# A two-layer graph kernel in batches: another order of the vector, scalar and GpSimd work for batches 0 to 3

## The chip, the cores and the metric

The kernel runs on one core of a Trainium2 chip. Its time is the device time of one execution in microseconds (us), the median of several executions; lower is better.

## The reference

```python
h = jnp.maximum(_layernorm(x, axis=-1), 0.0)          # x: (32, 256, 1024) float32
x = x + _L0_gnn_ref(h, adj, b1, adj, b2)               # adj: (256, 256), used as both weight matrices
...
    fv = x.mean(axis=1)                                # _construct_adj(h, 8), per batch
    nf = fv / norm(fv); sim = nf[:, :, None] * nf[:, None, :]
    _, idx = top_k(sim, 9); idx = idx[..., 1:]
    adj = zeros.at[b, row, idx].set(1.0); adj = max(adj, adj.T); adj[d, d] = 1
    ...
    h = relu(_gc(xr, adj, W1, b1)); h = _gc(h, adj, W2, b2)   # _gc: (adj / deg) @ (x @ W.T + b)
```

For each of 32 batches: layer norm and ReLU, a graph over the 1024 nodes built from the column means, and two graph convolutions with the same 256 x 256 weights, added to the input. The similarity is an outer product of one vector with itself, so a row of it picks either the largest or the smallest nodes; all nodes fall into 8 classes, and the graph is a small class-to-class table.

## The kernel before, in words

**Tiles.** A batch is two 128-row parts (`kf`, `m`) of 1024 columns, worked in two halves `h` of 512 columns. Float32 products are made from a high and a low part: `ps = w_hi*t_hi + w_lo*t_hi + w_hi*t_lo`, 8 matmuls in `product_hi` (L629) and 4 in `product_lo` (L635) for each half of each layer. The high part (`h_hi`, `r_hi`) is a ScalarE copy (`split_h` L366, `split_r` L403 and, for the very first half, L395), the low part (`h_lo`, `r_lo`) a GpSimd subtraction (L491, L502).

**One batch.** VectorE: statistics (`spreads` L761, `join` L768) and scale (`scales` L779, L782; `moments` is spreads and join). ScalarE: root of the variance (`root` L328), then the normalised `hb` (`normalise` L336). TensorE: `layer1`, then the graph's correction `masks` (L657, which reads the tile `onehot`). ScalarE: `relu` (L380 to L386), which also leaves column totals in `src2`. GpSimd: `products` (L481). VectorE: `class_terms` (L922). TensorE: `class_terms` (L688), VectorE: `table` (L928 to L934), which gives `tab`. TensorE: `layer2`, then `add_terms` (L664, reads `tab` and `onehot`). VectorE: `finish` (L943) adds bias and input, SyncE stores.

**Groups.** Batches go in groups of four that share the graph work: TensorE sums the columns of four normalised batches (`column_sums` L592; `first_sums` L579 for group 0), ScalarE copies the sums (`take_sums` L348 to L351) and makes the zero code (`zeros` L357 to L359, in the same PSUM tile `aux`), VectorE finds the top nodes (`top_first` L789 to `top_mark` L821), writes the class code (`codes` L827 to L831), `onehot` (L836) and its twin with the two 64-partition halves exchanged (`group_twin` L847, one call for each half), the degrees, factors, gathered rows, sources and biases (L856 to L915). GpSimd gathers rows of x by indirect DMA (`gather` L510) and builds `mix` (`tables`). `masks` of batches 0 and 1 need the first twin half of group 0, those of 2 and 3 the second.

**What sets the order.** Nothing is scheduled by a program. Each engine runs the calls in the order in which its function writes them, and semaphores hold an instruction until what it reads is there. From t = 3 on the loops repeat a fixed pattern with the statistics eight batches ahead; before that, batches 0 to 3 are written out by hand together with groups 0 and 1. TensorE's loop takes, for each t: `layer1(t+1, 0)` (with `class_terms(t)` between its two halves of products), `masks`, `add_terms(t, 0)`, `layer2(t, 1)`, `layer1(t+1, 1)`, `masks`, `add_terms(t, 1)`, `layer2(t+1, 0)`; for t = 0 the first `layer1` stands ahead of the loop, and `column_sums(1)` follows `add_terms(0, 1)`. `layer1(b, 1)` waits for `finish(b-1, 0)`, whose PSUM banks it takes over. `idle_products` (L696) are matmuls whose result nobody reads.

Of the kernel before, what the change touches and what calls it, by code (L numbers as in the profile page):

```python
# [19 lines left out]
H = 512  # L20
G = 4
# [71 lines left out]
def build(nc, x, x_t, w_t, b1, b2, small, staged, out):  # L93
# [5 lines left out]
    with ExitStack() as ctx:  # L99
# [225 lines left out]
        def _(act):  # L325
            def root(b):
                act.wait_ge(stats_ready, b + 1)
                nc.scalar.activation(std[:], mv[:, b % 2, :, 1], ACT.Sqrt, bias=eps[:]).then_inc(std_ready, 1)  # L328

            def normalise(b, kf):  # L330
                a, e = b % NH, b % RB
                if kf == 0:
                    act.wait_ge(norm_ready, b + 1)
                    if b >= NH:
                        act.wait_ge(hlo_ready, nth(b - NH, 1))
                last = nc.scalar.activation(  # L336
                    hb[:, a, kf], xin[:, b % NX, kf], ACT.Relu, bias=nmean[:, kf, e:e + 1],
                    scale=rstd[:, kf, e:e + 1], accum_out=h_tot[:, kf, e:e + 1])
# [15 lines left out]
            def zeros(k):  # L354
                com = dict(bias=half[:], scale=STEEP)
                act.wait_ge(fv_copied, 3 * k + 3)
                nc.scalar.activation(code[:, K_TOP + 1:H + 1], aux[:, K_TOP:H], ACT.Relu, **com)  # L357
                nc.scalar.activation(code[:, H + 1:N], aux[:, H:N - 1], ACT.Relu, **com)
                nc.scalar.activation(ZERO, aux[:, N - 1:N], ACT.Relu, **com).then_inc(zero_ready, 1)  # L359

            def split_h(b, h):
                n = half_of(h)
                act.wait_ge(h_ready, b + 1)
                if b > 0:
                    act.wait_ge(h_used, nth(b - 1, h))
                nc.scalar.activation(h_hi[:, :, n], hb[:, b % NH, :, n], ACT.Copy).then_inc(hhi_ready, 1)  # L366
# [53 lines left out]
            split_h(1, 1)  # L420
            normalise(5, 0)
            normalise(5, 1)
            first_unit()
            root(6)
            relu(0, 1, 0)
            relu(0, 1, 1)
            split_r(0, 1)
            normalise(6, 0)
            normalise(6, 1)

            for t in range(LAST):
                if t == 1:
                    normalise(LEAD + 1, 0)
                    normalise(LEAD + 1, 1)
                relu(t + 1, 0, 0)
                relu(t + 1, 0, 1)
                split_r(t + 1, 0)
                if t == 0:
                    root(7)
# [6 lines left out]
                if t == 0:  # L446
                    normalise(7, 0)
                    normalise(7, 1)
                    root(LEAD)
                if t == 1:  # L450
                    root(LEAD + 2)
                if 2 < t < NB - LEAD - 1:
# [4 lines left out]
                if t == 0:  # L457
                    take_sums(1)
                if t + 2 < NB:
                    split_h(t + 2, 1)  # L460
                if t == 0:
                    zeros(1)
                    normalise(LEAD, 0)
                    normalise(LEAD, 1)
                    root(LEAD + 1)
                elif t + LEAD + 1 < NB:
                    normalise(t + LEAD + 1, 0)
                    normalise(t + LEAD + 1, 1)
                if t == 1:
                    root(LEAD + 3)  # L470

        @block.gpsimd
        def _(pool):
# [72 lines left out]
            tables(0)  # L546
            split_h(1, 1)

            for t in range(-1, LAST):
                if t > 0 and (t + 1) % G == 0:  # L550
                    tables((t + 1) // G)
                if t == 1:
                    gather(1)
                split_r(t + 1, 0)
                if 1 < t < LAST - 1:
                    split_h(t + 2, 0, t + 1)
                else:
                    if t == 0:
                        split_h(2, 0)
                    products(t + 1)  # L560
                    if t == 1:
                        split_h(3, 0)
                split_r(t + 1, 1)
                if t >= 0 and t + 2 < NB:
                    split_h(t + 2, 1)
                if group_at(t, 0) is not None:
                    gather(group_at(t, 0))

        @block.tensor
        def _(pe):  # L570
# [182 lines left out]
        def _(dve):  # L753
# [220 lines left out]
            moments(6)  # L974
            spreads(7, 0)
            scales(6)
            spreads(7, 1)
            class_terms(0)
            join(7)
            spreads(8, 0)  # L980
            group_twin(0, 1)


            table(0)
            finish(0, 0)
            spreads(8, 1)
            scales(7)
            join(8)
            spreads(9, 0)
            spreads(9, 1)  # L990
            finish(0, 1)
            scales(8)
            join(9)
            spreads(10, 0)
            class_terms(1)
            spreads(10, 1)
            top_first(1)
            top_next(1)
            scales(9)
            join(10)  # L1000

            table(1)
            top_best(1)
            finish(1, 0)
            top_rows(1)
            spreads(11, 0)
            spreads(11, 1)
            finish(1, 1)
            scales(10)
            join(11)  # L1010
            top_mark(1)
            class_terms(2)

            table(2)
            finish(2, 0)
            codes(1)
            group_onehot(1)
            group_counts(1)
            group_twin(1, 0)
            group_twin(1, 1)  # L1020
            scales(11)
            finish(2, 1)
            group_degrees(1)
            group_factors(1)
            class_terms(3)
            group_gathered(1)
            group_sources(1)

# [64 lines left out]
```

## Time and profile before

| what | value |
|---|---|
| median of 3 executions | 502.77 us (502.76 to 504.25) |
| the profiled execution's own time | 504.29 us |
| its span, first to last instruction | 502.5 us |
| TensorE busy | 478.3 us (95%) |
| VectorE, ScalarE, GpSimd busy | 375.1, 350.0, 363.1 us (75%, 70%, 72%) |
| mean granted TensorE clock | 0.993 |

A span is what lies between the first and the last instruction; busy time is the union of an engine's instructions. "Idle before" in a row is how long the engine stood still just before it, and the releaser is the instruction for which it stood.

### The profile page before, as it was taken

What the parts mean: (1) busy time and instruction counts of PE and PEld (TensorE: products, weight loads), DVE (VectorE), ACT (ScalarE), POOL (GpSimd) and SP (SyncE); (2) the same over time, 40 slices, a digit from 0 to 9 for tenths busy, and PEclk for the clock granted to TensorE, in tenths of its full rate; (3) what the DMA queues carried; (4) which work ended last, traced back from release to release, by engine and by line L of the source; (5) the groups of instructions that cost most, each with busy time, mean ns of one, the idle gap of its engine ahead of it and who ended that gap; (6) DMA issues with size and microseconds to landing.
All of it is one profiled execution on the core that took longest, in us unless ns stands there. A gap on an engine that the chain in (4) does not pass through costs nothing.

```text
span 502.5 us, 7464 instructions
## 1 busy us (share of the span) xinstructions
PE 478.3 (95%) x2434; PEld 327.7 (65%) x2434; DVE 375.1 (75%) x956; ACT 350.0 (70%) x723; POOL 363.1 (72%) x343
## 2 busy tenths in 40 slices
PE   1997799899999999999999999999999999999996
PEld 0255556667776677767776677767777677777774
DVE  5989688988977898778877898878877675533334
ACT  4766698757877777777777777787777755556651
POOL 0356547957779687886888687896888687898883
PEclk9999799999999999999999999999999999999999
DMA  8992473556656465655656465664453244444424
GB/s 323 357 378 85 134 273 116 226 184 238 248 204 247 162 253 217 236 227 206 247 197 261 162 251 217 242 252 175 179 202 134 104 165 154 169 167 168 167 85 167
DMA packets 27718, 102.75 MB, mean 204 GB/s; under 512 B 2080, under 2 KB 2592, under 8 KB 27680
## 3 DMA queue, kind: packets, MB, share of 16 engines
q1 hardware_dynamic: 27296, 101.23, 53.5%
q0 software_dynamic: 384, 1.05, 0.6%
q8 instruction: 19, 0.31, 0.3%
q14 instruction: 19, 0.16, 0.1%
HBM read 68.72 MB, written 33.55 MB: 204 GB/s over the span
## 4 chain that ended last, share of the span: by engine, by line
PE 86%; DVE 5%; ACT 3%; DMA 3%; issue 1%; POOL 1%; SPq 0%; DVEq 0%; ACTq 0%; POOLq 0%
PE ps L629 48%; PE ps L635 22%; PE aux L592 5%; PE ps L657 4%; PE aux L688 3%; DMA xin<-x 2%; PE aux L616 1%; ACT hb L336 1%; PE aux L579 1%; DMA xg<-x_t,rows 1%; DVE res L943 1%; DVE onehot L847 1%; DVE stats L761 1%; PE aux L603 1%; POOL h_lo L491 1%
## 5 line engine op out<-in xcount | busy, mean ns | idle before, releaser
L502 POOL TENSOR_TENSOR r_lo<-r,r_hi 128x512 fp32r<-128x512 f32 x128 | 162.8, 1294 | 45.7 <-ACT r_hi L403 44.0
L491 POOL TENSOR_TENSOR h_lo<-hb,h_hi 128x512 fp32r<-128x512 f32 x128 | 164.0, 1295 | 7.5 <-ACT h_hi L366 7.4
L943 DVE SCALAR_TENSOR_TENSOR res<-ps,bias,res 128x512 f32<-128x512 f32 x128 | 90.1, 746 | 71.9 <-PE ps L664 71.9
L629 PE MATMUL ps<-r_hi,w_hi 128*128 128x512 f32 x256 | 109.0, 426 | 1.8 <-ACT r_hi L395 1.8
L629 PE MATMUL ps<-h_hi,w_hi 128*128 128x512 f32 x256 | 105.4, 412 | 0.4 <-DVE res L943 0.4
L629 PE MATMUL ps<-r_hi,w_lo 128*128 128x512 f32 x256 | 102.0, 399 | 0.0
L629 PE MATMUL ps<-h_hi,w_lo 128*128 128x512 f32 x256 | 101.0, 395 | 0.0
L336 ACT ACTIVATE hb<-xin,nmean,rstd 128x1024 f32<-128x1024 f32 x64 | 78.7, 1230 | 8.7 <-DVE nmean L782 8.7
L386 ACT ACTIVATE r<-ps,beta 128x512 f32<-128x512 f32 x64 | 43.4, 684 | 58.8 <-PE ps L657 56.5
L380 ACT ACTIVATE r<-ps,beta 128x504 f32<-128x504 f32 x64 | 43.5, 679 | 56.6 <-PE ps L657 52.3
L761 DVE BATCH_NORM_STATS2 stats<-xin 128x6 f32<-128x512 f32 x128 | 79.0, 677 | 3.6 <-DMA xin<-x 3.6
L635 PE MATMUL ps<-r_lo,w_hi 128*128 128x512 f32 x256 | 71.2, 400 | 0.0
L635 PE MATMUL ps<-h_lo,w_hi 128*128 128x512 f32 x256 | 70.2, 396 | 0.0
L403 ACT ACTIVATE r_hi<-r 128x1024 fp32r<-128x1024 f32 x63 | 66.8, 1061 | 2.4 <-PE ps L664 0.5
L629 PEld LDWEIGHTS ps<-r_hi,w_hi 128*128 128x128 f32 x256 | 48.5, 189 | 30.1 <-issue 12.9
L366 ACT ACTIVATE h_hi<-hb 128x1024 fp32r<-128x1024 f32 x64 | 67.0, 1047 | 0.0
L629 PEld LDWEIGHTS ps<-h_hi,w_hi 128*128 128x128 f32 x256 | 48.2, 188 | 17.8 <-issue 7.0
L635 PEld LDWEIGHTS ps<-r_lo,w_hi 128*128 128x128 f32 x256 | 48.4, 190 | 12.1 <-POOL r_lo L502 0.3
L635 PEld LDWEIGHTS ps<-h_lo,w_hi 128*128 128x128 f32 x256 | 48.1, 188 | 11.6
L629 PEld LDWEIGHTS ps<-h_hi,w_lo 128*128 128x128 f32 x256 | 48.3, 189 | 9.8
L629 PEld LDWEIGHTS ps<-r_hi,w_lo 128*128 128x128 f32 x256 | 48.7, 190 | 8.7
L481 POOL TENSOR_TENSOR prod<-src,mix 128x144 f32<-128x144 f32 x32 | 15.3, 478 | 48.8 <-issue 48.5
(100 smaller groups left out, 548.1 us busy)
## 6 DMA issues: line engine op xcount, KB each, us to landing
res<-x SPq DMA_DIRECT2D x32, 1024.0 KB, 4.9
out<-res SPq DMA_DIRECT2D x31, 1024.0 KB, 4.0
xin<-x SPq DMA_DIRECT2D x30, 1024.0 KB, 7.1
xin<-x SPq DMA_DIRECT2D x4, 512.0 KB, 5.0
out<-res SPq DMA_DIRECT2D x4, 256.0 KB, 2.1
w<-w_t SPq DMA_DIRECT2D x1, 256.0 KB, 9.0
cst<-small SPq DMA_DIRECT2D x1, 229.5 KB, 6.8
xg<-x_t,rows POOLq DMA_INDIRECT x8, 5.6
```

Of the source, the lines that this page charges most:

```text
L336: last = nc.scalar.activation(hb[:, a, kf], xin[:, b % NX, kf], ACT.Relu, bias=nmean[:, kf, e:e + 1], scale=rstd[:, kf, e:e + 1], accum_ou ...
L366: nc.scalar.activation(h_hi[:, :, n], hb[:, b % NH, :, n], ACT.Copy).then_inc(hhi_ready, 1)
L380: nc.scalar.activation(r[:, m, K_TOP:H], bank[m][:, K_TOP:H], ACT.Relu, accum_out=src2[:, m, e, C_COMMON:C_COMMON + 1], **com)
L386: last = nc.scalar.activation(r[:, m, H:N], bank[m][:], ACT.Relu, accum_out=src2[:, m, e, NCLS:NSRC], **com)
L403: nc.scalar.activation(r_hi[:, :, n], r[:, :, n], ACT.Copy).then_inc(rhi_ready, 1)
L491: last = nc.gpsimd.tensor_tensor(h_lo[:, kf, n], hb[:, b % NH, kf, n], h_hi[:, kf, n].bitcast(F32), ALU.subtract)
L502: last = nc.gpsimd.tensor_tensor(r_lo[:, kf, n], r[:, kf, n], r_hi[:, kf, n].bitcast(F32), ALU.subtract)
L592: last = nc.tensor.matmul(aux[32 * q:32 * q + 32, n], c_("ones")[:, 0:32], hb[:, (G * k + q) % NH, kf, n], start=(kf == 0), stop=(kf == KF ...
L629: nc.tensor.matmul(bank[m][:], wt[:, kf, m * P:m * P + P], mov[:, kf, n], start=(kf == 0 and wt is w_hi), stop=False, skip_group_check=True)
L635: last = nc.tensor.matmul(bank[m][:], w_hi[:, kf, m * P:m * P + P], mov[:, kf, n], start=False, stop=False, skip_group_check=True)
L761: last = nc.vector.bn_stats(stats[:, b % 2, kf, h], xin[:, a, kf, half_of(h)])
L943: nc.vector.scalar_tensor_tensor(res[:, b % NR, m, n], bank[m][:], bias2[:, m:m + 1], res[:, b % NR, m, n], ALU.add, ALU.add).then_inc(out ...
```

## The change

It touches batches 0 to 3 and groups 0 and 1; from t = 3 on every engine's order is as before. (In the changed file VectorE's lines are 43 higher, TensorE's 42 in the products, GpSimd's 35, ScalarE's 6.)

- The four `group_twin` calls of groups 0 and 1 leave VectorE; ScalarE makes these tiles by copying the other 64 partitions of `onehot` (`twin`).
- TensorE: in t = 0, `add_terms(0, 0)` moves from ahead of `layer2(0, 1)` to between its high and low products. Ahead of `layer2(0, 0)` there are four idle products of 256 columns instead of two, and two more behind its first two matmuls.
- ScalarE: `normalise(7)` moves ahead of `relu(1, 0)`, and `root`, `split_h`, `zeros` and `normalise` take other places.
- VectorE: statistics are dealt out otherwise; `table`, `finish` and the class work stand nearer to where they are read; `top_next` and `top_best` of group 1 go behind `finish(1, 0)`.
- GpSimd: `products(1)` goes ahead of `split_r(1, 1)`, `split_h(2)` behind it, and `gather(1)` behind `split_r(2, 1)` instead of ahead of `split_r(2, 0)`.

```diff
+            def twin(k, i):
+                act.wait_ge(counted, k + 1)
+                nc.scalar.activation(onehot[64 - 64 * i:128 - 64 * i, k % 2, 1], onehot[64 * i:64 * i + 64, k % 2, 0],
+                                     ACT.Copy).then_inc(onehot_ready, 1)
...
+            twin(0, 0)
             first_unit()
...
+            take_sums(1)
+            root(9)
+            split_h(2, 0)
+            split_h(2, 1)
+            zeros(1)
+            root(10)
+            twin(0, 1)
...
@@ GpSimd
+                split_r(t + 1, 1)
                 if t == 1:
                     gather(1)
...
@@ TensorE
                         if kf == 0 and m == 1 and rest is not None:
+                            idle_products(2, H // 2)
                             pe.wait_ge(rest, 1)
...
-            idle_products(2, H // 2)
+            idle_products(4, H // 2)
             layer2(0, 0)
...
                     masks(t + 1, 0)
+                    add_terms(t, 0)
+                    if group_at(t, 0) is not None:
+                        column_sums(group_at(t, 0))
+                    layer2(t, 1)
                 else:
                     terms()
-                add_terms(t, 0)
-                if group_at(t, 0) is not None:
-                    column_sums(group_at(t, 0))
-                layer2(t, 1)
+                    layer2(0, 1, lambda: add_terms(0, 0))
...
@@ VectorE
-            group_twin(0, 0)
+            spreads(6, 0)
             group_biases(0)
```

TensorE before, from the table's matmul of batch 0 on (`class_terms(0)`, `add_terms(0, 0)`, then `layer2(0, 1)`):

```order
L688 MATMUL aux<-w,src 24x128 x4
L664 MATMUL ps<-onehot,tab 128x512 x2
L629 MATMUL ps<-r_hi,w_hi 128x512
L629 MATMUL ps<-r_hi,w_lo 128x512
L629 MATMUL ps<-r_hi,w_hi 128x512
L629 MATMUL ps<-r_hi,w_lo 128x512
L629 MATMUL ps<-r_hi,w_hi 128x512
L629 MATMUL ps<-r_hi,w_lo 128x512
L629 MATMUL ps<-r_hi,w_hi 128x512
L629 MATMUL ps<-r_hi,w_lo 128x512
L635 MATMUL ps<-r_lo,w_hi 128x512 x4
```

The same place in the changed kernel:

```order
L730 MATMUL aux<-w,src 24x128 x4
L671 MATMUL ps<-r_hi,w_hi 128x512
L671 MATMUL ps<-r_hi,w_lo 128x512
L671 MATMUL ps<-r_hi,w_hi 128x512
L671 MATMUL ps<-r_hi,w_lo 128x512
L671 MATMUL ps<-r_hi,w_hi 128x512
L671 MATMUL ps<-r_hi,w_lo 128x512
L671 MATMUL ps<-r_hi,w_hi 128x512
L671 MATMUL ps<-r_hi,w_lo 128x512
L706 MATMUL ps<-onehot,tab 128x512 x2
L677 MATMUL ps<-r_lo,w_hi 128x512 x4
```

The two matmuls that read `tab` stand behind the eight high products.

VectorE before, from `class_terms(0)` to `finish(0, 0)`:

```order
L922 TENSOR_REDUCE src<-prod 128x48
L768 BN_AGGR mv<-stats 128x2 x2
L761 BN_STATS stats<-xin 128x6 x2
L847 TENSOR_SCALAR onehot,beside<-code_r,cst 64x1024
L928 CAST v_hi<-aux 128x128
L930 SCALAR_TENSOR_TENSOR aux<-v_hi,cst,aux 128x128
L932 CAST v_mid<-aux 128x128
L934 SCALAR_TENSOR_TENSOR tab<-v_mid,cst,aux 128x128
L943 SCALAR_TENSOR_TENSOR res<-ps,bias,res 128x512 x2
```

and now:

```order
L965 TENSOR_REDUCE src<-prod 128x48
L811 BN_AGGR mv<-stats 128x2 x2
L971 CAST v_hi<-aux 128x128
L973 SCALAR_TENSOR_TENSOR aux<-v_hi,cst,aux 128x128
L975 CAST v_mid<-aux 128x128
L977 SCALAR_TENSOR_TENSOR tab<-v_mid,cst,aux 128x128
L822 RECIPROCAL rstd<-std 128x2
L825 TENSOR_SCALAR nmean<-rstd,mv 128x1 x2
L986 SCALAR_TENSOR_TENSOR res<-ps,bias,res 128x512 x2
```

Two statistics and the twin are gone from ahead of the table; `scales(7)` stands behind it, ahead of `finish(0, 0)`.

ScalarE before, from `split_r(1, 1)` on (the sums of group 1, `split_h(2, 1)`, `zeros(1)`, batch 8):

```order
L403 ACTIVATE r_hi<-r 128x2x512
L348 ACTIVATE fv<-aux 128x512
L350 ACTIVATE fv<-aux 128x511
L351 ACTIVATE fv<-aux 128x1
L366 ACTIVATE h_hi<-hb 128x2x512
L357 ACTIVATE code<-aux,half 128x504
L358 ACTIVATE code<-aux,half 128x511
L359 ACTIVATE aux<-aux,half 128x1
L336 ACTIVATE hb,h_tot<-xin,nmean,rstd 128x1024 x2
```

and now:

```order
L409 ACTIVATE r_hi<-r 128x2x512
L348 ACTIVATE fv<-aux 128x512
L350 ACTIVATE fv<-aux 128x511
L351 ACTIVATE fv<-aux 128x1
L328 ACTIVATE std<-mv,eps 128x2
L372 ACTIVATE h_hi<-hb 128x2x512 x2
L357 ACTIVATE code<-aux,half 128x504
L358 ACTIVATE code<-aux,half 128x511
L359 ACTIVATE aux<-aux,half 128x1
L328 ACTIVATE std<-mv,eps 128x2
L364 ACTIVATE onehot<-onehot 64x1024
L336 ACTIVATE hb,h_tot<-xin,nmean,rstd 128x1024 x2
```

A root and one more half of `h_hi` now stand between the copied sums and the zeros, a root and the second twin half behind them.

## Rows read from the trace of the kernel before

**Rows 1.** The page: busy time of each engine, share of the span, instructions

```profile
PE 478.3 (95%) x2434; PEld 327.7 (65%) x2434; DVE 375.1 (75%) x956; ACT 350.0 (70%) x723; POOL 363.1 (72%) x343
```

**Rows 2.** Stretches of TensorE: busy us, matmuls, granted clock, DMA share, GB/s

```profile
0.00:103.90 103.90, 83.68 (x366) 0.97 0.63 231
150.00:497.00 347.00, 347.00 (x1823) 1.00 0.51 194
51.00:53.00 2.00, 0.00 (x0) 0.90 0.29 33
53.00:54.00 1.00, 0.76 (x3) 0.50 0.67 254
```

**Rows 3.** Timeline of TensorE, batch 0: start, us, line, count, idle before and releaser

```profile
42.85 1.13 PE L696 MATMUL aux<-hb,w 128*128 128x256 f32 x4
44.86 0.50 PE L629 MATMUL ps<-r_hi,w_hi 128*128 128x512 f32 x1 [0.87 <-ACT r_hi L395]
46.52 0.50 PE L629 MATMUL ps<-r_hi,w_hi 128*128 128x512 f32 x1 [0.93 <-ACT r_hi L395]
49.30 0.62 PE L688 MATMUL aux<-w,src 128*24 128x128 f32 x8 [0.18 <-DVE src L922]
53.24 0.61 PE L664 MATMUL ps<-onehot,tab 24*128 24x512 bf16 x2 [3.32 <-DVE tab L934]
59.06 0.57 PE L629 MATMUL ps<-h_hi,w_hi 128*128 128x512 f32 x1
```

**Rows 4.** Timeline of VectorE ahead of that table, and the first finish

```profile
50.59 1.28 DVE L847 TENSOR_SCALAR_CACHE_REDUCE onehot<-code_r,cst 64x1024 bf16<-64x1024 bf16 x1
51.80 0.28 DVE L928 CAST v_hi<-aux 128x128 bf16<-128x128 f32 x1
52.83 0.35 DVE L934 SCALAR_TENSOR_TENSOR tab<-v_mid,cst,aux 128x128 bf16<-128x128 bf16 x1
53.95 1.41 DVE L943 SCALAR_TENSOR_TENSOR res<-ps,bias,res 128x512 f32<-128x512 f32 x2 [0.77 <-PE ps L664]
```

**Rows 5.** Timeline of TensorE, group 1's sums and batches 1 to 3

```profile
62.46 3.64 PE L592 MATMUL aux<-hb,cst 128*32 128x512 f32 x32
69.95 0.62 PE L688 MATMUL aux<-w,src 128*24 128x128 f32 x8
72.57 0.39 PE L657 MATMUL ps<-onehot,mask 24*128 24x512 bf16 x2
73.76 0.39 PE L664 MATMUL ps<-onehot,tab 24*128 24x512 bf16 x2 [0.80 <-DVE tab L934]
76.97 0.40 PE L629 MATMUL ps<-h_hi,w_hi 128*128 128x512 f32 x1
79.87 0.39 PE L657 MATMUL ps<-onehot,mask 24*128 24x512 bf16 x2
79.88 0.39 PE L664 MATMUL ps<-onehot,tab 24*128 24x512 bf16 x2
97.52 0.47 PE L629 MATMUL ps<-h_hi,w_hi 128*128 128x512 f32 x1 [0.44 <-DVE res L943]
99.66 0.62 PE L688 MATMUL aux<-w,src 128*24 128x128 f32 x8 [0.98 <-DVE src L922]
```

**Rows 6.** Timeline of ScalarE: a root, a half of h_hi and the zeros of group 1, batch 4

```profile
46.37 0.28 ACT L328 ACTIVATE std<-mv,eps 128x2 f32<-128x2 f32 x1
66.71 1.06 ACT L366 ACTIVATE h_hi<-hb 128x1024 fp32r<-128x1024 f32 x1
67.66 0.69 ACT L357 ACTIVATE code<-aux,half 128x504 bf16<-128x504 f32 x1
68.79 0.25 ACT L359 ACTIVATE aux<-aux,half 128x1 f32<-128x1 f32 x1
103.79 0.68 ACT L380 ACTIVATE r<-ps,beta 128x504 f32<-128x504 f32 x1 [4.33 <-DVE beta L915]
```

**Rows 7.** Timeline of GpSimd: the low part of r for batch 0's second half

```profile
49.15 2.50 POOL L502 TENSOR_TENSOR r_lo<-r,r_hi 128x512 fp32r<-128x512 f32 x2 [0.55 <-ACT r_hi L403]
```

More of the change, by code:

```diff
@@ L428, in _ @@
             normalise(6, 0)
+            root(7)
             normalise(6, 1)
[L431 to L434, printed above, removed]
+            normalise(7, 0)
+            normalise(7, 1)
+            relu(1, 0, 0)
+            relu(1, 0, 1)
+            split_r(1, 0)
+            root(8)
+            relu(1, 1, 0)
+            relu(1, 1, 1)
+            split_r(1, 1)
+            take_sums(1)
[5 more added lines that the diff above has]
+            twin(0, 1)
+            normalise(8, 0)
+            normalise(8, 1)
+            relu(2, 0, 0)
+            relu(2, 0, 1)
+            split_r(2, 0)
+            split_h(3, 0)
+            normalise(9, 0)
+            relu(2, 1, 0)
+            relu(2, 1, 1)
+            split_r(2, 1)
+            split_h(3, 1)
+            normalise(9, 1)
+            normalise(10, 0)
+            relu(3, 0, 0)
+            relu(3, 0, 1)
+            split_r(3, 0)
+            split_h(4, 0)
+            normalise(10, 1)
+            relu(3, 1, 0)
+            relu(3, 1, 1)
+            root(11)
+            split_r(3, 1)
+            split_h(4, 1)
+            twin(1, 0)
+            normalise(11, 0)
+            normalise(11, 1)
+            twin(1, 1)
+            for t in range(3, LAST):
                 relu(t + 1, 0, 0)
@@ L437, in _ @@
                 split_r(t + 1, 0)
-                if t == 0:
-                    root(7)
                 if group_at(t, 0) is not None:
@@ L445, in _ @@
                     zeros(group_at(t, 0))
[L446 to L452, printed above, removed]
+                if t < NB - LEAD - 1:
                     root(t + LEAD + 1)
@@ L456, in _ @@
                 split_r(t + 1, 1)
-                if t == 0:
-                    take_sums(1)
                 if t + 2 < NB:
                     split_h(t + 2, 1)
[L461 to L466, printed above, removed]
+                if t + LEAD + 1 < NB:
                     normalise(t + LEAD + 1, 0)
                     normalise(t + LEAD + 1, 1)
-                if t == 1:
-                    root(LEAD + 3)
         @block.gpsimd
@@ L547, in _ @@
             split_h(1, 1)
-            for t in range(-1, LAST):
-                if t > 0 and (t + 1) % G == 0:
-                    tables((t + 1) // G)
+            split_r(0, 0)
+            products(0)
+            split_r(0, 1)
+            split_r(1, 0)
+            products(1)
+            split_r(1, 1)
+            split_h(2, 0)
+            split_h(2, 1)
+            for t in range(1, LAST):
+                if (t + 1) % G == 0:
+                    tables((t + 1) // G)
+                split_r(t + 1, 0)
+                if t < LAST - 1:
+                    split_h(t + 2, 0, t + 1)
+                else:
+                    products(t + 1)
+                split_r(t + 1, 1)
                 if t == 1:
                     gather(1)
[L554 to L564, printed above, removed]
+                if t + 2 < NB:
                     split_h(t + 2, 1)
@@ L971, in _ @@
             group_sources(0)
-            group_twin(0, 0)
+            spreads(6, 0)
             group_biases(0)
-            moments(6)
+            spreads(6, 1)
+            join(6)
             spreads(7, 0)
@@ L979, in _ @@
             join(7)
+            table(0)
+            scales(7)
+            finish(0, 0)
             spreads(8, 0)
-            group_twin(0, 1)
-            table(0)
-            finish(0, 0)
             spreads(8, 1)
-            scales(7)
             join(8)
             spreads(9, 0)
-            spreads(9, 1)
             finish(0, 1)
             scales(8)
+            spreads(9, 1)
             join(9)
@@ L995, in _ @@
             class_terms(1)
+            top_first(1)
+            scales(9)
             spreads(10, 1)
-            top_first(1)
-            top_next(1)
-            scales(9)
             join(10)
             table(1)
+            scales(10)
+            finish(1, 0)
+            top_next(1)
             top_best(1)
-            finish(1, 0)
             top_rows(1)
+            finish(1, 1)
+            class_terms(2)
+            top_mark(1)
+            table(2)
             spreads(11, 0)
[L1007 to L1014, printed above, removed]
             finish(2, 0)
@@ L1018, in _ @@
             group_counts(1)
-            group_twin(1, 0)
-            group_twin(1, 1)
+            spreads(11, 1)
+            join(11)
+            finish(2, 1)
+            class_terms(3)
             scales(11)
-            finish(2, 1)
             group_degrees(1)
             group_factors(1)
-            class_terms(3)
             group_gathered(1)
```

## Prediction, made before the changed kernel ran

> **What bounds the kernel now.** The page's busy times come first [rows 1]: TensorE works 95% of the span, the three others 70 to 75%, so a gain must come from TensorE's idle time or from its clock, and another engine's work counts only where TensorE stands for it. The stretches say where that is [rows 2]: from 150 to 497 us TensorE is busy for 347.00 of 347.00 us at full clock, while in the first 103.90 us it is busy for 83.68, which leaves 20.2 us idle. About half of that is the start, before the first matrix is there; the change leaves it alone. The rest is in batches 0 to 3, where the change is, and TensorE's timeline with its releasers gives it piece by piece: 0.87 and 0.93 us for ScalarE's r_hi, 3.32 us for VectorE's tab [rows 3], then 0.80 for tab, 0.44 for the finish of batch 2, 0.98 for the class sources of batch 3 [rows 5]. The clock matters too: in the wait for tab it falls from 1.00 to 0.50 of full speed, that is from 2.4 to 1.2 GHz [rows 2], and it is low for all of the unit of work that follows. As nothing in the loops is changed from t = 3 on and TensorE never waits there, a microsecond won or lost on TensorE before the fourth batch should arrive at the end unchanged. That is the frame of the sum.
>
> **The wait for tab, and the half clock.** TensorE finishes class_terms(0) at 49.30 + 0.62 = 49.92, and VectorE could start on the table then. It doesn't: statistics and a twin half stand in its queue, and the table runs from 51.80 to 52.83 + 0.35 = 53.18, 1.38 us [rows 4]. The change does two things here. VectorE has the table next, so tab is there at about 49.97 + 1.38 = 51.4. And TensorE doesn't wait for tab but does layer2(0, 1)'s eight high products first. They need r_hi of that half, which is there when GpSimd begins on it at 49.15; the low products need r_lo, ready at 49.15 + 2.50 = 51.65 [rows 7]. The same unit at full clock, terms and twelve products, takes 76.97 - 73.76 = 3.21 us [rows 5], its last third (four low products) about 0.95. So high products run from 49.92 to about 51.9, the terms find tab ready, and the low products find r_lo ready. The wait of **3.32** us is gone. So is the half clock, if it followed from that wait: the unit took 59.06 - 53.24 = 5.82 us [rows 3] against 3.21, which gives **2.61**.
>
> **Idle products.** Two of 256 columns begin at 42.85, and a pair lasts 1.13 us with its tail; two more end at about 45, just where r_hi arrives (44.86), and the pair behind the first two matmuls lies in the 0.93 us before 46.52 [rows 3]. They fill idle time: 0, at most 0.2 us of delay, and nothing gained unless the clock is spared by them.
>
> **The later waits.** In batch 1 the masks start at 72.57 and the terms at 73.76, while where tab is in time the two start together (79.87 and 79.88) [rows 5]. Tab was late by its own queue: the table of batch 1 follows statistics, roots and searches. In the new order VectorE has two statistics fewer to do there, joins are done earlier, and by my walk tab(1) is ready about half a microsecond before the masks. Gain 73.76 - 72.57 = **1.18**. The search of group 1 now goes behind finish(1, 0), the two twins (1.28 us each, as in [rows 4]) go to ScalarE and statistics of batch 11 are split around them, so finish(2, 1) and the sources of batch 3 come before TensorE asks: **0.44** and **0.98** gone. In the walk the sources are there 1.8 us ahead, the finish only some 0.5. Total removed: 3.32 + 2.61 + 1.18 + 0.44 + 0.98 = 8.53.
>
> **What is late next.** (1) layer1(1, 1) takes over the banks of finish(0, 0). Before, that finish (1.41 us, [rows 4]) lay beside layer2(0, 1). Now the terms that release it come late in the same unit: they end at 49.92 + 3.21 - 0.95 = 52.2, VectorE ends at about 53.65, TensorE asks at 53.13. With a semaphore's delay **0.55** us of wait; bounds 0 (its first matrix starts it earlier) and 1.4 (all of the finish). (2) class_terms(1) writes aux, so it waits for zeros(1). From the start T of group 1's column sums TensorE needs 69.95 - 62.46 = 7.49 us to reach it [rows 5]. ScalarE has copied the sums at T + 66.71 - 62.46 = T + 4.25; then come a root (0.28 at most), two halves of h_hi (0.95 each, 66.71 to 67.66) instead of one, and the zeros (67.66 to 69.04, 1.38) [rows 6]: T + 7.81. The wait is 0.32 and a semaphore, I take **0.4**; bounds 0 and 1.0, as ScalarE, which now has all of batch 7's normalising ahead of batch 1, could itself come late to the sums. (3) The biases of group 1 keep their place behind table(3), and the short wait of ScalarE and TensorE for beta stays.
>
> **The twin on ScalarE.** No row shows a copy of 64 x 1024 bf16. The nearest is L366's copy of 128 x 1024, 1.06 us; bounds 0.69 (half the columns, L357) and 1.28 (VectorE's). I take 1.06. The first falls before relu(0, 0), where ScalarE waits for TensorE; the last two fall where it stood 4.33 us before 103.79 [rows 6]. The one that can be felt is twin(0, 1), which masks(2, 0) needs: it ends near T + 9.2, TensorE asks at T + 7.89 + 72.57 - 69.95 = T + 10.5. Cost 0. The Trainium skill ("ScalarE: Activation LUTs", Rules for kernel authors) speaks against this move: in bf16 VectorE should be up to three times faster per element on such simple operations. The row has it otherwise: the form used here, with its sum, takes 1.28 us on VectorE, no less than ScalarE's copy. By the rule a third of 1.28, some 0.4, would be enough there, two twins would free VectorE of 0.9 us instead of 2.6, and the 1.8 us by which the sources of batch 3 are early would shrink to almost nothing: the sum would be the same or a few tenths less.
>
> **GpSimd.** gather(1) moves behind split_r(2, 1) and split_h(3, 1) moves behind the gather; both are read several microseconds later, and VectorE delivers the row numbers about when the queue gets there. Cost 0; if a gather came late, transposes in layer2(3, 0) would wait, which is a part of the third case below.
>
> **The sum.** 8.53 removed, 0.95 added: 7.6 us. Against its own span 502.5 - 7.6 = 494.9. The profiled execution took 504.29 us and lies 1.5 above the median of 502.77; the median is what is predicted, and 502.77 - 7.6 = **495.1 us**.
>
> **The rivals.**
> *The half clock stays, once.* TensorE's activity around 44 to 50 us is thin anyway [rows 3], and the clock could fall there or at the new wait at 53.1. Against it: gaps of 0.87, 0.93, 0.80 and 0.98 left it at 1.00 and only 3.32 us without work brought it down. Price: a unit at half clock, 2.6 us: 497.7.
> *Slower: short gaps bring the clock down each time.* This is one mechanism at the new waits near 53, 64 and at the beta wait. Each fall costs a unit at half clock, 2.6 us. Three give 7.8 and eat the gain (502.9); at a fourth, the first waits of batch 0, the kernel is slower, 505.5. The traced gaps speak against it. The Trainium skill ("TensorE: Matmul & The Clock Gate", A second HAM failure mode) describes such a kernel, where frequent small idle times between groups of matmuls made the clock swing; by that rule this case would rank higher, but the gaps of the trace don't bear it out.
> *A new wait in batches 1 to 3.* ScalarE or VectorE comes late by what the walk has wrong: twin(0, 1) past its 1.3 us, finish(2, 1) past its 0.5, a late gather. Price 1 to 3 us in all, say 2: 497.1.
> *No waits are added at all*: finish and zeros come in time, 494.1.
>
> **How the numbers follow.** Forecast 0.60 (494.3 to 496.3), nothing added 0.10, half clock once 0.10, a new wait 0.15, slower or level by the clock 0.05. The two shown clusters of executions are 1.5 us apart, which widens the top a little. Range 493.5 to 498.3: the low end is the sum without added waits and with a little more, the top a half-clock unit and half a microsecond. 0.3% is 1.5 us, about what a measurement of this kernel can tell from no change; every case but the clock's is below 501.3. Faster 0.95, same 0.02, slower 0.03.
>
> **What would show it.** Right: TensorE's row for tab in batch 0 without idle before it, granted clock 1.00 from 44 us on, a wait for a finish of about 0.5 us before layer1(1, 1), one of 0.4 for the zeros ahead of class_terms(1), no waits at the terms of batch 1 or the sources of batch 3, and group 2's column sums beginning near 96.3 where they began at 103.9 (the end of the first stretch in [rows 2]). TensorE should then be busy without a break as before. Wrong: any row of TensorE with over 1 us of idle after 50 us, a clock of 0.5 anywhere behind it, or new idle time in the loop from batch 4 on.

## The result, and the profile after

| | before | changed |
|---|---|---|
| median | 503.12 us (5 executions, 502.76 to 504.25) | 497.23 us (5 executions, 496.20 to 497.76) |
| ratio | | 0.9875, 95% interval 0.9863 to 0.9887 |
| profiled execution, its span | 504.29, 502.5 us | 497.13, 495.3 us |
| mean granted clock in it | 0.993 | 1.000 |

The change makes the kernel faster by 1.25%, 6.3 us (5.7 to 6.9) by the ratio; the two medians are 5.9 us apart. The forecast was 495.1 us in a range of 493.5 to 498.3, a gain of 7.6 us.

The page and the stretches of TensorE in the changed kernel (us busy, matmuls, clock, DMA share, GB/s), against [rows 1, 2]:

```profile
PE 476.9 (96%) x2442; PEld 327.1 (66%) x2442; DVE 371.3 (75%) x948; ACT 354.4 (72%) x727; POOL 364.2 (74%) x343
```

```profile
0.00:96.79 96.79, 82.31 (x374) 1.00 0.66 248
96.79:150.00 53.21, 53.21 (x276) 1.00 0.62 231
150.00:490.00 340.00, 340.00 (x1790) 1.00 0.51 192
```

Idle time ahead of group 2's column sums fell from 20.2 to 14.5 us, the clock stays at 1.00 in this execution (the other four have means of 0.997 to 0.999), and behind that point TensorE is busy without a break, as before. So what was won by then reached the end. TensorE's timeline of the changed kernel, the rows that answer to [rows 3, 5]:

```profile
49.64 0.62 PE L730 MATMUL aux<-w,src 128*24 128x128 f32 x8 [0.18 <-DVE src L965]
52.25 0.39 PE L706 MATMUL ps<-onehot,tab 24*128 24x512 bf16 x2
54.30 0.47 PE L671 MATMUL ps<-h_hi,w_hi 128*128 128x512 f32 x1 [0.53 <-DVE res L986]
65.44 0.62 PE L730 MATMUL aux<-w,src 128*24 128x128 f32 x8 [0.29 <-ACT aux L359]
68.06 0.39 PE L706 MATMUL ps<-onehot,tab 24*128 24x512 bf16 x2
94.92 1.08 PE L657 MATMUL aux<-src,w 128*128 128x32 f32 x8 [0.16 <-DVE src L942]
96.79 3.64 PE L633 MATMUL aux<-hb,cst 128*32 128x512 f32 x32 [0.18 <-DVE beta L958]
```

The wait for tab in batch 0 is gone, and so are those for batch 1's tab (68.06), for finish(2, 1) (0.44) and for batch 3's class terms (0.98). New are the waits for finish(0, 0) (0.53) and for the zeros (0.29), and one of 0.16 at the sources of group 1; the one at its biases is 0.18, where it was 0.43. From class_terms(0) to group 2's column sums it took 103.91 - 49.30 = 54.61 us before and takes 96.79 - 49.64 = 47.15 now: 7.46 us less. Of this, 5.10 us are won up to layer1(1, 1) (59.06 - 49.30 against 54.30 - 49.64) and 2.36 us behind it. The start was 0.34 us slower in this execution than in the profiled one of before.

VectorE's table and first finish, against [rows 4]:

```profile
50.31 0.29 DVE L971 CAST v_hi<-aux 128x128 bf16<-128x128 f32 x1 [0.54 <-PE aux L730]
51.35 0.35 DVE L977 SCALAR_TENSOR_TENSOR tab<-v_mid,cst,aux 128x128 bf16<-128x128 bf16 x1
52.74 1.41 DVE L986 SCALAR_TENSOR_TENSOR res<-ps,bias,res 128x512 f32<-128x512 f32 x2 [0.59 <-PE ps L706]
```

and ScalarE's first twin, its two halves of h_hi, the end of the zeros, and the second twin, against [rows 6]:

```profile
39.66 1.05 ACT L364 ACTIVATE onehot<-onehot 64x1024 bf16<-64x1024 bf16 x1
62.02 2.00 ACT L372 ACTIVATE h_hi<-hb 128x1024 fp32r<-128x1024 f32 x2
65.05 0.25 ACT L359 ACTIVATE aux<-aux,half 128x1 f32<-128x1 f32 x1
66.36 1.06 ACT L364 ACTIVATE onehot<-onehot 64x1024 bf16<-64x1024 bf16 x1
```

VectorE now waits for TensorE ahead of the table, where it used to begin the table 1.9 us after TensorE's last product. The twin copy takes 1.05 us on ScalarE, the 1.06 of the nearest row.

### The profile page after: what moved, and what is told of

It is laid out like the page before. It is cut to its first block, busy times and chain, and to the rows that moved or that the text cites. A ratio compares the mean times of both kernels' runs of the same rounds, so it can differ in the third digit from the quotient of the medians.

```text
span 495.3 us, 7476 instructions
## 1 busy us (share of the span) xinstructions
PE 476.9 (96%) x2442; PEld 327.1 (66%) x2442; DVE 371.3 (75%) x948; ACT 354.4 (72%) x727; POOL 364.2 (74%) x343
## 3 DMA queue, kind: packets, MB, share of 16 engines
q0 software_dynamic: 384, 1.05, 0.5%
## 4 chain that ended last, share of the span: by engine, by line
PE 82%; DVE 7%; ACT 4%; DMA 3%; issue 2%; POOL 1%; SPq 0%; DVEq 0%; ACTq 0%; POOLq 0%
PE ps L671 46%; PE ps L677 21%; PE aux L633 4%; PE ps L699 4%; PE aux L730 3%; DVE stats L804 2%; DMA xin<-x 2%; DVE res L986 1%; ACT hb L336 1%; PE aux L620 1%; PE aux L657 1%; DMA xg<-x_t,rows 1%; POOL h_lo L526 1%; PE aux L644 1%; ACT h_hi L372 1%
```

## The experiments

Ratios are to the kernel before, timed in the same session on the same chip. The runs lie in three sessions on three chips, and the changed kernel was timed in a session of its own (ratio 0.9875), so it is compared with the others through these ratios. A tenth of a per cent is 0.5 us. Each kernel ran 4 to 12 times.

**before_again**: no edit.

> The kernel before, unchanged, to see several of its executions with span and clock. Theory A (the gain of the change differs from the sum because the half-clock stretch in batch 0 is not equally long in every execution): mean granted clocks spread, say 0.993 to 1.000, and the executions with the higher clock are shorter by up to 2.6 us. Theory B (the spread comes from the start, from when the first loads land): the clock is the same in all, the spans differ by the start alone. Ratio to the kernel before 1.000.

Ratio 0.9999 (0.9986 to 1.0011). Twelve executions have spans from 500.6 to 503.3 us and mean clocks from 0.991 to 0.996. The four longest have 0.991, the eight others 0.993 to 0.996. Its profiled execution (span 501.2) is not the one that the prediction read. TensorE's timeline and stretches in it:

```profile
44.78 0.50 PE L629 MATMUL ps<-r_hi,w_hi 128*128 128x512 f32 x1 [0.87 <-ACT r_hi L395]
46.45 0.50 PE L629 MATMUL ps<-r_hi,w_hi 128*128 128x512 f32 x1 [0.93 <-ACT r_hi L395]
53.16 0.39 PE L664 MATMUL ps<-onehot,tab 24*128 24x512 bf16 x2 [2.02 <-DVE tab L934]
```

```profile
45.00:50.00 5.00, 4.07 (x11) 0.69 0.00 0
50.00:53.00 3.00, 1.14 (x10) 0.95 0.11 11
53.00:56.00 3.00, 2.84 (x8) 0.61 0.85 339
56.00:60.00 4.00, 4.00 (x16) 0.86 0.00 0
```

Here the clock fell twice: first behind the two waits of 0.87 and 0.93 us, then behind the wait for tab. The first fall cost nothing, since TensorE's slow work filled part of the time in which it would have waited: 2.02 us of wait instead of 3.32, and the terms begin at 53.16, where they began at 53.24 [rows 3]. The second fall cost less than the one in the first profile, since full speed came back sooner: layer1(1, 1) begins at 57.92, 4.76 us after the terms, not 5.82. This is 1.06 of the 1.3 us between the two spans. Against the 3.21 us of a unit at full clock, the half clock cost 1.55 us here and 2.61 there.

```profile
57.92 0.40 PE L629 MATMUL ps<-h_hi,w_hi 128*128 128x512 f32 x1
```

Theory A holds in that the falls differ between executions. The mean clock doesn't give the span (0.993 goes with 502.5 us in the first profile and with 501.2 here): a fall in front of a wait costs less than one behind it, and the mean also counts the end of the span, where TensorE has finished. In codes_early, below, no fall comes before 490 us, and yet its mean is 0.998:

```profile
492.00:494.50 2.50, 0.00 (x0) 0.58 0.64 242
```

How much of the spread of 2.7 us comes from the start (theory B) stays open, as only two of these executions have a trace.

**gap_filled**: idle products in the wait, written to banks that the next unit overwrites.

```diff
                 else:
                     terms()
+                    idle_beside(7)
                 add_terms(t, 0)
```

`idle_beside` (its definition is left out here) waits for r_hi of batch 0's second half and issues the given number of matmuls of 256 columns into the first bank of `pair2(0, 1)`.

> The kernel before, with seven idle products of 256 columns (some 3.15 us) put into TensorE's 3.3 us wait for tab in batch 0; nothing else. If the half clock follows from the wait, the clock stays at full speed and the unit behind it takes 3.2 us instead of 5.8: 2.6 us less, ratio 0.995, although the wait itself is as long as before. Rival (the clock falls on its own account around there, or the unit is slow for another reason): no change, ratio 1.000. If the idle products delay the terms, up to 0.3 us of it is lost.

Ratio 0.9968 (0.9956 to 0.9981): 1.6 us (1.0 to 2.2). The profiled execution has clock 1.000. Of the ten, seven have 0.999 to 1.000 and spans of 499.4 to 500.0 us, three have 0.997 and 501.1 to 501.3; these three have no trace. The clock is a term of its own, worth 1.6 us over all executions and not 2.6, which agrees with the 1.55 of the second profile. TensorE still can't go on before tab is there; seven products that nobody needs fill that time.

**terms_inside_only**: only TensorE's edit in t = 0 (the last TensorE part of the diff shown above).

> The kernel before, with TensorE's edit alone: add_terms(0, 0) between the high and the low products of layer2(0, 1). VectorE still delivers tab at 53.2, so TensorE works from 49.9 to 51.9 and waits 1.3 us instead of 3.3; the clock should hold. Gain 2.0 of waiting and 2.6 of half clock, less a wait of about 1 us for finish(0, 0) ahead of layer1(1, 1): some 3.7 us, ratio 0.993. Rival (the 1.3 us wait still brings the clock down): 1 us or less.

Ratio 0.9953 (0.9938 to 0.9968), 2.4 us, not 3.7. The wait for tab came as expected, the one for finish(0, 0) was half as long (0.53 instead of about 1), and the clock fell:

```profile
53.43 0.39 PE L664 MATMUL ps<-onehot,tab 24*128 24x512 bf16 x2 [1.25 <-DVE tab L935]
55.48 0.52 PE L629 MATMUL ps<-h_hi,w_hi 128*128 128x512 f32 x1 [0.53 <-DVE res L944]
```

```profile
55.00:56.00 1.00, 0.52 (x2) 0.89 1.02 418
56.00:59.00 3.00, 3.00 (x9) 0.50 0.02 5
```

In this execution two short waits close together, 1.25 and 0.53 us, were enough; two of the six have 0.999 and 1.000. So the edit on TensorE alone gives somewhat over a third of the change. Whether VectorE's new order or the added idle products are what keeps the clock in the change isn't shown by this run, as it has neither.

**no_idle_products**: the changed kernel without the idle products around layer2(0, 0).

```diff
-                            idle_products(2, H // 2)
...
-            idle_products(4, H // 2)
```

> The changed kernel without the four and the two idle products around the first matmuls of layer2(0, 0). If they only fill time in which TensorE waits for ScalarE, the time is that of the changed kernel (ratio 0.9875) or 0.1 us less. Rival (they are what keeps the clock up): gaps of 2.6 and 0.9 us stand there, the clock falls, and 1 to 3 us are lost, ratio 0.990 to 0.993.

Ratio 0.9903 (0.9887 to 0.9919), 1.4 us worse than the change, with intervals that just touch; all five executions have 0.992 or 0.994. Two waits of 1.93 and 0.76 us stand there. The clock falls behind the first of them, before the second begins, and is half for what follows:

```profile
44.35 0.50 PE L670 MATMUL ps<-r_hi,w_hi 128*128 128x512 f32 x1 [1.93 <-ACT r_hi L401]
46.01 0.79 PE L670 MATMUL ps<-r_hi,w_hi 128*128 128x512 f32 x1 [0.76 <-ACT r_hi L401]
```

```profile
44.00:45.00 1.00, 0.65 (x2) 0.88 0.00 0
45.00:50.00 5.00, 4.24 (x10) 0.50 0.00 0
50.00:53.00 3.00, 3.00 (x16) 0.74 0.25 22
```

**before_idle_products**: the same products put into the kernel before.

```diff
+                            idle_products(2, H // 2)
                             pe.wait_ge(rest, 1)
...
-            idle_products(2, H // 2)
+            idle_products(4, H // 2)
```

> The kernel before with the idle products of the change alone: four ahead of layer2(0, 0) and two behind its first two matmuls. If the clock in the kernel before falls in some executions already at the 0.87 and 0.93 us waits for r_hi (as in the second profile of it, near 46 us), this takes that fall away and leaves the one at the wait for tab; as the first fall lies partly in the shadow of the wait for tab, the gain is small: 0 to 0.7 us, ratio 0.9985 to 1.000. Rival (the idle products carry the gain of the change): ratio 0.995 or less.

Ratio 1.0008 (0.9995 to 1.0021). With the wait for tab behind them they bring nothing: in this trace too the clock falls in that wait of 3.32 us (0.64 in the stretch from 52 to 53 us, 0.50 from 53 to 56). They are worth 1.4 us in the changed kernel, which has no such wait.

**terms_ahead**: the changed kernel with add_terms(0, 0) ahead of layer2(0, 1).

```diff
-                    layer2(0, 1, lambda: add_terms(0, 0))
+                    add_terms(0, 0)
+                    layer2(0, 1)
```

> The changed kernel with add_terms(0, 0) back ahead of layer2(0, 1). TensorE then waits from 50.3 to 51.7 for tab (1.4 us), without a fall of the clock; finish(0, 0) comes earlier, so the wait of 0.5 us ahead of layer1(1, 1) goes. Loss 0.9 us against the changed kernel, ratio 0.989. Rival (the clock falls in the 1.4 us): loss 3 us or more, ratio 0.994.

Ratio 0.9882 (0.9868 to 0.9897), which isn't resolved from the change's own. Its profiled execution shows a wait of 1.50 us for tab and then a fall:

```profile
51.00:52.00 1.00, 1.00 (x6) 0.98 0.00 0
52.00:55.00 3.00, 3.00 (x9) 0.50 0.96 321
```

In that trace the way from class_terms(0) (48.60) to group 2's sums (97.76) takes 49.16 us, 2.0 more than in the changed kernel. The start was 1.04 us quicker in the same execution, which hides half of it. The other three executions have 0.998 and 0.999, too high for a stretch as long as this one (over 3 us at half clock), so that the fall is the exception there. The expected 0.9 is inside the interval, and the rival's 3 us isn't, though the fall that it named did come once; the size between 0 and 1.1 stays open.

**gather_ahead**: GpSimd's gather back ahead of split_r(2, 0).

```diff
+                if t == 1:
+                    gather(1)
                 split_r(t + 1, 0)
...
                 split_r(t + 1, 1)
-                if t == 1:
-                    gather(1)
```

> The changed kernel with gather(1) back ahead of split_r(2, 0) in GpSimd's queue. VectorE gives the row numbers at 75.0, so r_lo(2, 0) is ready at 78.6 instead of 75.7, and TensorE, which asks at 76.5, waits 2 us: ratio 0.992. Rival (the gather's place is without effect, something else is late there anyway): ratio 0.9875 as the changed kernel.

Ratio 0.9915 (0.9902 to 0.9928), 2.0 us worse, as expected. TensorE's row says for what:

```profile
78.25 2.02 PE L677 MATMUL ps<-r_lo,w_hi 128*128 128x512 f32 x4 [2.30 <-POOL r_lo L537]
```

In this execution the clock fell behind that wait too (mean 0.996); the four others have 1.000 and took 0.6 to 0.9 us less.

VectorE's long operation of codes(1), of which more below, happens to fall into a pause of GpSimd here:

```profile
86.36 1.21 DVE L870 SCALAR_TENSOR_TENSOR code_r<-fv,code 128x1015 bf16<-128x1015 f32 x1
```

```profile
83.55 2.52 POOL L526 TENSOR_TENSOR h_lo<-hb,h_hi 128x512 fp32r<-128x512 f32 x2
88.26 2.56 POOL L537 TENSOR_TENSOR r_lo<-r,r_hi 128x512 fp32r<-128x512 f32 x2 [2.19 <-ACT r_hi L409]
```

**twins_back**: group 1's two twin halves made by VectorE again.

```diff
             group_counts(1)
+            group_twin(1, 0)
+            group_twin(1, 1)
             spreads(11, 1)
```

> The changed kernel with the two twin halves of group 1 made by VectorE again, behind group_counts(1). Each takes 1.28 us there; in the changed kernel the sources come 0.16 us late for TensorE as it is, so the full 2.6 us are added ahead of them: ratio 0.993. Rival (there is slack in VectorE's queue there, as the prediction had it with 1.8 us): at most 0.8 us, ratio 0.989.

Ratio 0.9932 (0.9919 to 0.9945), 2.9 us worse, about the length of both (2.55 us). The wait that grows is that for finish(2, 1), which stands behind them in VectorE's queue, ahead of the sources; the sources themselves then come in time:

```profile
93.12 0.67 PE L669 MATMUL ps<-h_hi,w_hi 128*128 128x512 f32 x1 [2.18 <-DVE res L984]
```

So finish(2, 1) had about 0.4 us to spare in the changed kernel (2.55 - 2.18). The clock fell behind that wait in this execution (0.50 from 94 to 96 us), but the one execution with 1.000 took no less than the others (500.13 us against a median of 500.30).

**both_waits** takes the two new waits away; **bank_by_bank** has the first of its edits alone.

```diff
+                        if kf == 0 and m == 1 and second is not None:
+                            pe.wait_ge(out_ready, second)
...
+                elif b == 1 and h == 1:
+                    pe.wait_ge(out_ready, 1)
                 elif b > 0 and h == 1:
                     pe.wait_ge(out_ready, 2 * nth(b - 1, 0))
...
             split_h(2, 0)
-            split_h(2, 1)
             zeros(1)
+            split_h(2, 1)
```

> The changed kernel with two of its own new waits taken away: layer1(1, 1) waits for the first bank of finish(0, 0) only and for the second ahead of its third matmul, and zeros(1) goes ahead of split_h(2, 1) on ScalarE. If the waits are what the rows say (0.53 and 0.29 us) and nothing takes their place, 0.8 us less than the changed kernel, ratio 0.986. Rival (the time is handed to the next wait, sources or biases of group 1, whose VectorE queue is full from 83 us on): 0.3 us or less.

Ratio 0.9959 (0.9944 to 0.9973): 4.2 us slower than the change. Both waits are gone from TensorE's rows (one of 0.23 us for twin(0, 1) takes the place of a part), and the loss comes some 30 us later. VectorE's main operation of codes(1) took 3.02 us in the changed kernel and takes 6.75 here:

```profile
82.33 6.75 DVE L874 SCALAR_TENSOR_TENSOR code_r<-fv,code 128x1015 bf16<-128x1015 f32 x1
```

GpSimd in the same stretch:

```profile
81.70 2.56 POOL L526 TENSOR_TENSOR h_lo<-hb,h_hi 128x512 fp32r<-128x512 f32 x2
84.21 2.53 POOL L537 TENSOR_TENSOR r_lo<-r,r_hi 128x512 fp32r<-128x512 f32 x2
86.70 1.29 POOL L526 TENSOR_TENSOR h_lo<-hb,h_hi 128x512 fp32r<-128x512 f32 x1
88.27 1.12 POOL L516 TENSOR_TENSOR prod<-src,mix 128x144 f32<-128x144 f32 x1 [0.28 <-issue]
```

and ScalarE's r_hi(3, 0), which the pair at 84.21 reads:

```profile
82.74 1.06 ACT L409 ACTIVATE r_hi<-r 128x1024 fp32r<-128x1024 f32 x1
```

GpSimd runs five subtractions without a pause, from 81.70 to 87.99. VectorE's operation, begun at 82.33 by the trace, ends at 89.08, 1.1 us after the pause begins. In the changed kernel the same two engines look like this:

```profile
82.97 3.02 DVE L870 SCALAR_TENSOR_TENSOR code_r<-fv,code 128x1015 bf16<-128x1015 f32 x1
```

```profile
82.35 2.56 POOL L526 TENSOR_TENSOR h_lo<-hb,h_hi 128x512 fp32r<-128x512 f32 x2
84.86 3.53 POOL L537 TENSOR_TENSOR r_lo<-r,r_hi 128x512 fp32r<-128x512 f32 x2
```

```profile
83.70 1.06 ACT L409 ACTIVATE r_hi<-r 128x1024 fp32r<-128x1024 f32 x1
```

There r_hi(3, 0) is ready at 84.76, just as GpSimd gets to it (84.86); VectorE gets through between GpSimd's two pairs (the seam, below), and GpSimd's second pair is 1.0 us longer instead. In both_waits r_hi is ready at 83.80, 0.4 us before GpSimd gets to it: ScalarE is earlier by more than GpSimd, the seam closes, and VectorE stands until the next pause. Four traces go together here: a margin of 0.1 us and 3.02 us of operation in the changed kernel and in twins_back, 0.4 us and over 6.7 in both_waits and bank_by_bank. No run moves r_hi alone, so that its timing decides at the seam is argued from these four. Late counts then cost 0.64 and 0.89 us on TensorE, a late finish(2, 1) 1.47, and the clock falls:

```profile
93.76 0.77 PE L673 MATMUL ps<-h_hi,w_hi 128*128 128x512 f32 x1 [1.47 <-DVE res L990]
```

```profile
94.00:95.00 1.00, 1.00 (x3) 0.50 0.48 193
```

The fall isn't the main loss: three of the six executions have a clock of 1.000 and still took 500.95 to 501.36 us, the three others 501.90 to 502.68.

> The changed kernel with layer1(1, 1) waiting for finish(0, 0) bank by bank, the other wait left as it is. TensorE is 0.5 us earlier from 54 us on. If codes(1) keeps its 3 us, ratio 0.9865; if ScalarE's earlier r_hi takes away the gap between GpSimd's subtractions, the operation takes 5 us or more and the ratio is 0.992 or more. The theory of a race against that gap allows both and says that the time follows the length of that one operation; the rival says that time and that length have nothing to do with one another.

Ratio 0.9946 (0.9930 to 0.9962), and the operation takes 6.76 us. This edit alone closes the seam: r_hi(3, 0) is ready at 84.37, and GpSimd gets to it at 84.79.

**codes_early** and **both_waits_codes**: codes(1) moved on VectorE, in the changed kernel and in both_waits.

```diff
             table(2)
-            spreads(11, 0)
+            codes(1)
             finish(2, 0)
-            codes(1)
+            spreads(11, 0)
             group_onehot(1)
```

> The changed kernel with codes(1) on VectorE moved from behind finish(2, 0) to behind table(2), and spreads(11, 0) from ahead of finish(2, 0) to behind it. Theory (the long operation of codes(1), 3.0 us in the changed kernel and 6.75 us with both waits taken away, is held back by GpSimd's subtractions and gets through where GpSimd pauses): started near 80.5 it falls into the pause in which GpSimd issues the gather (81.2 to 82.3) and takes 1.2 to 2 us; the sources' and biases' waits of 0.16 and 0.18 us go: ratio 0.9868, 0.3 us less than the changed kernel. Rival (the operation is slow for what it reads, wherever it stands): still 3 us, ratio 0.9875.

Ratio 0.9845 (0.9832 to 0.9859), median 496.32 us. The operation is held for the last 0.7 us of a subtraction pair and then falls beside the gather, where GpSimd has no subtraction running:

```profile
80.07 1.79 DVE L870 SCALAR_TENSOR_TENSOR code_r<-fv,code 128x1015 bf16<-128x1015 f32 x1
```

```profile
78.24 2.54 POOL L537 TENSOR_TENSOR r_lo<-r,r_hi 128x512 fp32r<-128x512 f32 x2
80.94 1.80 POOL L545 DMA_INDIRECT xg<-x_t,rows  x1 [0.16 <-issue]
```

> Both waits taken away as before, and codes(1) moved as in the kernel beside it. Theory (GpSimd's hold on that one operation was the whole loss of 4.4 us): the operation takes 1.2 to 2 us, no clock falls near 92, and the time is 0.8 to 1.1 us below the changed kernel: ratio 0.9855. Rival (one of the two edits costs by itself, such as half of h_hi too late): ratio 0.992 or more, as with both edits alone.

Ratio 0.9849 (0.9835 to 0.9863), median 496.57. With the operation in the pause, the same two edits that had cost 4.2 us cost nothing: the hold of GpSimd on it was the loss. They bring no more than 0.1 us over codes_early, though: from class_terms(0) to group 2's sums it is 46.62 us against 46.73, and 47.15 in the changed kernel. What they save comes back as a wait of 0.23 us for twin(0, 1) at masks(2, 0), one of 0.17 at class_terms(2), and small delays at the sources and biases. The expected ratio, 0.9855, is inside the interval, but the trace has only 0.53 us less than the changed kernel's where 0.8 to 1.1 was expected. Of the lower median of codes_early, 0.9 us below the changed kernel's, 0.38 is the start in the traced pair; codes_early is the fastest version found, with an interval that only just clears that of the change.

## Why the prediction was right, and where it was off

**The frame** held: nothing from group 2's sums on changed, and the 7.46 us won ahead of them are, but for 0.1 us, what the profiled spans show once the start is set apart (502.5 - 495.3 = 7.2, plus 0.34 of slower start). The sum of 7.6 us was right for this pair of executions, piece by piece: 5.38 was forecast up to layer1(1, 1) (3.32 + 2.61 - 0.55) and 5.10 measured, 2.20 behind it (1.18 + 0.44 + 0.98 - 0.40) and 2.36 measured.

**The wait for tab and the half clock** held in the profiled pair: no idle time at the terms of batch 0, clock 1.00. The term that was mis-sized is the half clock: taken alone it gave 1.6 us and not 2.61 (gap_filled), since its price differs between executions, 2.61 in the one that I had read and 1.55 in the second profile (before_again).

**The idle products** were costed at nothing, and gained nothing unless they spare the clock. They do: 1.4 us (no_idle_products). The step "they fill idle time" missed that the change leans on them.

**The new waits**: finish(0, 0) 0.53 against 0.55, zeros 0.29 against 0.4. Tab of batch 1 was ready at 67.49, 0.56 us ahead of the masks, as in the walk, and finish(2, 1) came in time, with 0.4 us to spare by twins_back, where the walk had 0.5.

**The sources of batch 3**, which class_terms(3) reads, came in time, but the walk had too much to spare. TensorE gets to them at about 92.0 (its row starts at 92.08, without a wait), and VectorE has them ready at 91.04:

```profile
90.45 0.59 DVE L965 TENSOR_REDUCE src<-prod 128x48 f32<-128x432 f32 x1
```

That is 1.0 us and not 1.8. The wait of 0.16 us stands at another tile, the sources of group 1 (L942), which the prediction didn't price; in the trace of before they were 0.9 us early. (The expectation of twins_back takes the one for the other.) The missing 0.8 us has the size of what codes(1) grew by: 3.02 us where the trace of before has 2.30. The prediction doesn't ask what set that length:

```profile
88.80 2.30 DVE L827 SCALAR_TENSOR_TENSOR code_r<-fv,code 128x1015 bf16<-128x1015 f32 x1
```

Beside idle GpSimd it takes 1.21 (gather_ahead). In the trace of before GpSimd's subtraction pair that began at 87.48 ends at 90.02, and the operation ends 1.08 us after it.

**The twin's rule.** The copy took 1.05 us on ScalarE and each half 1.27 or 1.28 us on VectorE (twins_back), so the row was the right guide for the form that this kernel uses. No run makes the twin by a plain copy on VectorE, so what that would take isn't shown.

**GpSimd's move** cost nothing, as forecast, but it isn't free to leave out: with the gather back ahead of split_r(2, 0) the changed kernel loses 2.0 us (gather_ahead). The prediction named no such gain.

**From spans to medians** is the step that failed in size. Every execution's time is its span plus 1.8 us (504.29 and 502.5, 497.13 and 495.3). The profiled execution of before has a span of 502.5 in a spread from 500.6 to 503.3. Against the second profile (501.2) it isn't its longer wait that makes it slower, as tab came at the same time in both, but the unit behind it, 5.82 us instead of 4.76. I subtracted the gain read from it, 7.6 us, from a median of three that belongs to quicker executions, and the quicker one that has a trace has 1.06 us less to gain. Against its own time the sum gives 504.29 - 7.6 = 496.7, near the 497.13 measured; against the median it gave 495.1, where 497.23 was measured. That the range still held this is owed to its width at the top, which had been set mostly for one unit at half clock, and so is partly luck.

**The rivals.** The half clock didn't stay in the profiled execution, but in variants it fell at waits of 1.25 and 0.53 us, of 1.50 and of 1.93, so that case deserved more than its 0.10. Of the further waits that it feared in batches 1 to 3 none above 0.2 us came in the change, and both_waits shows how near a longer one was.

## What to carry to other kernels

Read the same kernel's profile more than once before a gain is subtracted: a clock fall whose place and price vary between executions made the sum right for one execution (7.46 of 7.6 us) and wrong for the median, so set the sum against that execution's own time. Ask of every operation whose length differs between its occurrences what stood beside it, since a queue that fits by the lengths of an older trace may rest on one seam in another engine. Here idle products paid only where no longer wait followed them, and taking two short waits away cost 4.2 us until the held operation had been moved. Don't read falls of the clock from a span's mean alone: it also counts the end, after the last matmul.

## What the runs showed of the hardware

- A VectorE operation with two SBUF tensors (code_r, 128 x 1015) takes 1.21 us beside idle GpSimd, 2.30 in the kernel before, 3.02 in the change, 6.75 and 6.76 where GpSimd's two-tensor subtractions follow one another without a pause. It isn't slowed but held: in the kernel before, in codes_early, both_waits and bank_by_bank it ends 1.1 us after GpSimd's instruction or run of instructions, whenever it began. GpSimd is held in turn: a pair of 2.53 us took 3.53, products of 0.49 us took 1.12, an indirect DMA of 1.02 us took 1.80. The Trainium skill ("SBUF — State Buffer", SBUF: two separate sides) says that the two engines share a pair of ports as an exclusive lock, and that the one that starts first keeps it for its whole instruction while the other fully blocks. The rows agree, and add that in both_waits and bank_by_bank a run of GpSimd instructions kept VectorE out across all of the seams between them.
- The granted clock fell to one half (1.2 GHz) in or behind single waits of 1.50 (terms_ahead), 1.93 (no_idle_products), 2.02 (before_again), 2.18 (twins_back), 2.30 (gather_ahead) and 3.32 us (before, before_idle_products), and behind short waits close together (0.87 and 0.93; 1.25 and 0.53; 0.64, 0.89 and 1.47). In other executions the pair of 0.87 and 0.93 left it at 2.4 GHz, and three of the four executions of terms_ahead have a mean too high for such a fall. The same kernel's first fall came near 47 us in one execution and in the stretch from 52 to 53 in another.
- What a fall costs depends on its place: in front of a wait for another engine, the slow work eats into the wait (3.32 us became 2.02, and the terms behind it began no later); behind it, a unit of 3.2 us took 4.8 or 5.8.
